# Fourth self attention without a maximum, its transposed scores in two pairs of PSUM banks in turn

## The reference, cut to what matters

```python
x = x + _L3_attn_ref(_layernorm(x, axis=-1), ...)

def _L3_attn_ref(x, Wq, bq, Wk, bk, Wv, bv, Wo, bo):
    SCALE = 1.0 / np.sqrt(D_K * 2.0)
    TEMP = 1.5
    ...
    q = _l2norm(heads(Wq, bq))
    k = _l2norm(heads(Wk, bk))
    v = heads(Wv, bv)
    scores = jnp.einsum('bhqd,bhkd->bhqk', q, k) * SCALE
    scores = jnp.clip(scores, -5.0, 5.0)
    causal = jnp.triu(jnp.ones((T, T), dtype=bool), k=1)
    scores = jnp.where(causal[None, None], -10000.0, scores)
    attn = jax.nn.softmax(scores / TEMP, axis=-1)
    out = jnp.einsum('bhqk,bhkd->bhqd', attn, v)
    out = out.transpose(0, 2, 1, 3).reshape(B, T, D)
    return (out @ Wo.T + bo) * 0.5
```

## Time and profile before

| | us |
|---|---|
| median of 3 runs | 5149.49 |
| the runs | 5117.75, 5149.49, 5162.92 |
| span of the profiled execution | 5139.5 |

### The profile page before, as it was taken

One profiled execution on the slowest core, in us unless ns is written; L12 is line 12 of the kernel. 1 busy time (PEld: TensorE's weight loads), 2 busy tenths in 40 slices (PEclk: granted clock), 3 DMA queues, 4 the chain that ended last, 5 costly groups with the idle time before them and its releaser, 6 DMA issues. The chain is left out here.

```text
span 5139.5 us, 86857 instructions
## 1 busy us (share of the span) xinstructions
PE 4115.3 (80%) x26550; PEld 2846.4 (55%) x26550; DVE 2994.6 (58%) x4577; ACT 2115.7 (41%) x3227; POOL 1733.6 (34%) x1171
## 2 busy tenths in 40 slices
PE   8899999999979988778789999994763434336699
PEld 4588888888867746534445555552432222223377
DVE  4344445444523444446545676656459999996433
ACT  3255555555522232124324555542235555551122
POOL 2266666666524232004310000000225555541033
PEclk8799999999969988799867999996876666667699
DMA  2000000000002203220022222210010101000011
GB/s 85 1 10 19 10 19 19 19 10 19 10 1 62 59 1 91 48 61 2 1 56 47 65 62 62 62 33 1 1 24 18 26 17 26 17 19 1 0 61 48
DMA packets 124607, 152.80 MB, mean 30 GB/s; under 512 B 86912, under 2 KB 110224, under 8 KB 124080
## 3 DMA queue, kind: packets, MB, share of 16 engines
q1 hardware_dynamic: 124208, 147.72, 11.5%
HBM read 109.43 MB, written 2.66 MB: 22 GB/s over the span
## 5 line engine op out<-in xcount | busy, mean ns | idle before, releaser
L989 POOL TENSOR_TENSOR pexp_lo<-arena,pexp_hi 128x800 fp32r<-128x800 f32 x384 | 635.7, 1655 | 443.2 <-POOLq L988 442.5
L2173 DVE TENSOR_REDUCE arena<-ps 100x1 f32<-100x482 f32 (+1 forms) x768 | 489.9, 657 | 266.8 <-DVEq L2160 256.5
L2053 DVE TENSOR_REDUCE arena<-ps 128x1 f32<-128x482 f32 (+3 forms) x624 | 392.9, 656 | 365.6 <-DVEq L2031 354.8
L1330 ACT ACTIVATE arena<-ps 128x800 f32<-128x800 f32 x384 | 322.3, 839 | 500.3 <-ACTq L1328 497.8
L2471 DVE MATCH_REPLACE8 arena<-arena 100x1444 f32<-100x1444 f32 x256 | 420.8, 1656 | 0.0
L1420 ACT ACTIVATE arena<-ps 128x800 f32<-128x800 f32 x384 | 315.5, 837 | 249.8 <-ACTq L1419 243.6
L3202 PE MATMUL ps<-kst,qs 96*100 96x482 f32 (+1 forms) x768 | 376.2, 492 | 43.0 <-PEq L3156 39.4
L935 POOL TENSOR_TENSOR max_diag<-w_const,arena 100x800 fp32r<-100x800 f32 x160 | 246.8, 1543 | 436.5 <-POOLq L933 436.5
L3331 PE MATMUL ps<-w_const,w_cross 100*128 100x100 f32 x192 | 43.2, 380 | 374.1 <-PEq L3328 374.1
L1331 ACT ACTIVATE pexp_hi<-ps 128x800 fp32r<-128x800 f32 x384 | 319.5, 832 | 0.0
L2573 DVE TENSOR_TENSOR arena<-ps,arena 128x400 f32<-128x400 f32 x256 | 147.1, 575 | 280.2 <-DVEq L2572 280.2
(11 more groups left out here) (393 smaller groups left out, 9621.0 us busy)
## 6 DMA issues: line engine op xcount, KB each, us to landing
ctxT<-in_ctxT SPq DMA_DIRECT2D x56, 541.5 KB
kst<-mid SPq DMA_DIRECT2D x128, 180.5 KB, 3.1
ctxk<-in_ctx SPq DMA_DIRECT2D x40, 528.0 KB
chunk<-in_ff_chunks SPq DMA_DIRECT2D x77, 193.0 KB, 2.4
arena<-gate_dram SPq DMA_DIRECT2D x64, 200.0 KB, 3.8
kst<-xn SPq DMA_DIRECT2D x64, 180.5 KB, 2.9
arena<-gate_dram SPq DMA_DIRECT2D x64, 100.0 KB, 2.6
arena<-in_ctxT SPq DMA_DIRECT2D x8, 541.5 KB
```

Source lines behind the costliest of these rows:

```text
L989: own(nc.gpsimd.tensor_tensor(pexp_lo[p % 3][:, :, :], pexp[p % 3], pexp_hi[p % 3][:, :, :], ALU.subtract))
L1330: nc.scalar.activation(pexp[p % 3], of, ACT.Exp, scale=scale).then_inc(s.pexp_ready, 1)
L2053: peak = nc.vector.tensor_reduce(mparts[0:at.stop - at.start, m, c:c + 1], bank(k, z - a, at.stop - at.start), AX.X, ALU.max)
L2173: peak = nc.vector.tensor_reduce(mparts2[:, h, c:c + 1], bank(k, z - a, S), AX.X, ALU.max)
```

## The change

Where `cfg["unit"]` is set, GpSimd leaves its part of the stage out, VectorE makes no `k_diag` and no maxima, and TensorE has a list of its own: value rows first, then in each step the values of step t - 1, the masks and transposed scores of step t + 1 (`bounded_score`, into banks 0 and 1 or 2 and 3 in turn, where ScalarE's exponent reads them), and the side work behind them. The dummies of a unit stand ahead of its first scores. The other three self attentions keep their code.

```diff
--- before.py
+++ after.py
@@ -644,6 +644,9 @@
 
     UNREAD_FIRST, UNREAD = 14, 8
 
+    def score_bank(cfg, t):
+        return 2 * (t % 2) if cfg.get("unit") else 4
+
     CHUNKS = [(0, 482), (482, 962), (962, K)]
     SCORE_BANKS, SUM_BANKS = (0, 1, 3), (2, 4)
 
@@ -918,6 +921,8 @@
 
         def self_attention(n):
             nsm = SELF[SA[n]]["nsm"]
+            if SELF[SA[n]].get("unit"):
+                return
             ident = W("const", "ident")[0:S, 0:S].unsqueeze(1).to_broadcast([S, 8, S])
 
             def own(ins):
@@ -1247,7 +1252,8 @@
                     roots()
                 act.wait_ge(s.scoresT, 1)
                 act.sem_inc(s.scoresT, -1)
-                nc.scalar.activation(probsT[:, t % 2, :].rearrange("p (c t) -> p c t", c=2), ps[0:S, 4:6, 0:GT], ACT.Exp,
+                of = score_bank(cfg, t)
+                nc.scalar.activation(probsT[:, t % 2, :].rearrange("p (c t) -> p c t", c=2), ps[0:S, of:of + 2, 0:GT], ACT.Exp,
                                      scale=float(cfg["scale"])).then_inc(s.probsT_ready, 1)
                 if t % 2 == 0 and t > 0:
                     keep(t // 2 - 1)
@@ -1759,7 +1765,9 @@
                 nc.vector.tensor_scalar(col[:, 7:8], W(wst, "gate_b"), -1.0, None, ALU.mult).then_inc(s.dve_done, 1)
                 dve.wait_ge(s.dve_done, 1)
                 dve.sem_inc(s.dve_done, -1)
-            dve.sem_inc(s.stage_pool, 1)
+            bounded = cfg.get("unit")
+            if not bounded:
+                dve.sem_inc(s.stage_pool, 1)
             dve.sem_inc(s.stage_act, 1)
             dve.sem_inc(s.stage_pe, 1)
             cols = W("const", "head_cols")
@@ -1805,7 +1813,7 @@
                     else:
                         done(nc.vector.tensor_copy(to, bank(i % 8)))
                     dve.sem_inc(s.heads_read, 1)
-                if i == 1:
+                if i == 1 and not bounded:
                     for j in range(4):
                         k_diagonal(0, j)
             if cfg.get("gate"):
@@ -1871,11 +1879,12 @@
                     done(nc.vector.tensor_tensor(xd, of, xd, ALU.add))
                     dve.sem_inc(s.proj_free, 1)
 
-            for t in range(3):
-                maxima(t)
+            if not bounded:
+                for t in range(3):
+                    maxima(t)
             for t in range(8 * units):
                 u, k = divmod(t, 8)
-                if k < 4 and u + 1 < units:
+                if k < 4 and u + 1 < units and not bounded:
                     k_diagonal(u + 1, k)
                 kind, G, i = beside(nsm, t)
                 if kind == "project":
@@ -1884,7 +1893,7 @@
                     by_roots(u // nsm - 1)
                 elif step_behind(nsm, t) == 5:
                     by_weights(u // nsm - 1)
-                if t + 3 < 8 * units:
+                if t + 3 < 8 * units and not bounded:
                     maxima(t + 3)
                 if t % 2 == 1 and t >= 3:
                     normalise(t // 2 - 1)
@@ -2755,7 +2764,18 @@
 
                 par, sm, half, at, own = place_of(t)
                 r = slice(32 * (half + c), 32 * (half + c) + 32)
-                return mm(bank(4 + c, GT, S), k_rows[sm][r, at], q_diag[par][r, :, own], start=False, stop=True)
+                return mm(bank(score_bank(cfg, t) + c, GT, S), k_rows[sm][r, at], q_diag[par][r, :, own], start=False, stop=True)
+
+            def bounded_score(t):
+
+                if t % 8 == 0:
+                    pe.wait_ge(s.q_diag_ready, 1)
+                    pe.sem_inc(s.q_diag_ready, -1)
+                    unread(UNREAD if t > 0 else UNREAD_FIRST)
+                for c in range(2):
+                    mm(bank(score_bank(cfg, t) + c, GT, S), id_bf, causalT_bf[:, :], start=True, stop=False)
+                scoreT(t, 0)
+                scoreT(t, 1).then_inc(s.scoresT, 1)
 
             def values(t):
                 u, k = divmod(t, 8)
@@ -2813,6 +2833,39 @@
                 score(t, 0)
                 score(t, 1).then_inc(s.scores, 1)
 
+            if cfg.get("unit"):
+                for i in range(4):
+                    value_rows(0, i, VALUE_BANKS[i])
+                pe.wait_ge(s.v_ready, 4)
+                pe.sem_inc(s.v_ready, -4)
+                bounded_score(0)
+                for t in range(8 * units):
+                    kind, G, i = beside(nsm, t)
+                    if t > 0:
+                        pe.wait_ge(s.probsT_ready, 1)
+                        pe.sem_inc(s.probsT_ready, -1)
+                        values(t - 1)
+                    if t + 1 < 8 * units:
+                        bounded_score(t + 1)
+                    if kind == "features":
+                        features(G, i)
+                    elif kind == "project":
+                        project()
+                    elif kind == "values":
+                        side_bank()
+                        value_rows(G, i, 7)
+                    if t % 2 == 1 and t >= 3:
+                        gathered(t // 2 - 1)
+                pe.wait_ge(s.probsT_ready, 1)
+                pe.sem_inc(s.probsT_ready, -1)
+                values(8 * units - 1)
+                pe.wait_ge(s.o_kept, 1)
+                pe.sem_inc(s.o_kept, -1)
+                gathered(4 * units - 1)
+                for c in range(nsm):
+                    features(NG - 1, c)
+                project()
+                return
             pe.wait_ge(s.k_diag_ready, 1)
             pe.sem_inc(s.k_diag_ready, -1)
             first_score(0)
```

## The result

| | before | after |
|---|---|---|
| median, 13 runs each | 5148.82 us | 5165.09 us |
| lowest, highest | 5111.75, 5270.82 | 5145.61, 5220.11 |
| span of the profiled execution | 5139.5 us | 5158.2 us |

The ratio is 1.0071 with the interval [1.0043, 1.0099]: the changed kernel is slower, by 22 to 51 us. The comparison leaves out executions far above a kernel's fastest (the profiled ones of e1, e2 and e5 further down are among these), so a ratio need not be the quotient of two medians.

What follows compares the result with a forecast made beforehand. The loop was taken as bound by what TensorE streams. Start −7.6, steps −22.3, waits gone −4, new waits +7.0 and the falling clock +22.5 made −4.4 us: 5145 from 5149.5, range 5112 to 5177.

Steps and rivals of the forecast that it cites:

- the clock is low in plain steps too: Rival: whole loop low from its first wait, dummies giving back about a quarter of 68 us; 5173 us, chance 0.16.
- held clock: Rival: TensorE keeps 2.4 GHz over the loop's new waits, so all 27 us stay; 5123 us, chance 0.22.
- the sum: Whole stage at full clock: start, steps and waits that go or come together save 26.9 us.
- the price for a loop wholly at half clock: All loop steps, value rows, gatherings and dummies at 1.2 GHz: 68 us more.
- plain steps: Loop steps counted without side work: values, masks and scores, 1.77 us instead of 2.48, and 1.46 more at 1.2 GHz.
- Part 1: Ahead of the loop: shorter VectorE chain and new order let step 1 begin 7.6 us earlier, clock returning at the dummies' end.
- Part 3: Clock falls behind features in units 2 to 4 and returns with dummies in units 2 and 3; costs 22.5 us.
- Part 2: Loop steps: shorter steps save 22.3 us, waits that go 4 us, waits that come cost 7.0 us.
- the prediction's trap: Loop scores: both pairs run side by side, so removing one pair saves no time; a pair alone takes about 0.85 us.
- The waits: Gatherings wait for bank 7 behind features (1.14 us) and project (1.2 us), three of each, 7.0 us.

Runs made afterwards that it cites:

- e1: The changed kernel with 26 instead of 14 dummies ahead of the stage's first scores; ratio to the kernel before 1.0000.
- e2: e1 with four more dummies ahead of the masks in every step; ratio to the kernel before 1.0004.
- e5: The changed kernel with features and project in bank 5, features copied behind that step's exponent, dummies in bank 4; ratio to the kernel before 0.9950.
- e9: e6 with VectorE's update behind normalise and an empty exponent on ScalarE to load the table early; ratio to the kernel before 0.9933.
- e10: e9 with no dummies at the later units; ratio to the kernel before 0.9898.
- e6: e5 with 26 first dummies instead of 14; ratio to the kernel before 0.9918.
- e7: The changed kernel with 26 first dummies and 20 instead of 8 at each later unit; ratio to the kernel before 0.9998.
- e8: e5 with 26 dummies at the start and none later; ratio to the kernel before 0.9980.
- e4: The kernel before with no dummies in this stage; ratio to the unaltered kernel before 0.9995.
- e3: The changed kernel with no dummies in this stage; ratio to the kernel before 1.0062.

## Why the prediction was wrong

The forecast was a gain of 4.4 us and the outcome a loss; what happened is the rival "the clock is low in plain steps too", in the form in which dummies give a part back. That rival was put at 5173, 24 us slower, and the part is 25.1 us longer. That the sizes agree is in part luck: at a held clock the loop gains some 9 us more than the sum (below), and the dummies gave back some 8 us (an estimate: e5's 173.1 and the new waits of 5.9, less 170.8) where a quarter of 68, 17 us, was put. Right was the price for a loop wholly at half clock, 68 us: e5 (all low) is 66.5 us above e9 (held), and 69.2 if the 12 dummies that e9 has more (7.36 − 4.67 = 2.7 us, by the starts in e1 and after) are taken off. Its condition was not right: it let plain steps lose the clock, and e1 and e10 show that they hold it.

**The step that failed** is in Part 1: "I take it to come back at the end of the dummies again", and its copy in Part 3, "to come back with the dummies at the unit's end". I took two rises, seen once each, for what 14 and 8 dummies always bring. A window of before, and the first matmul of the step behind the dummies of the earlier trace rows:

```profile
3641.00:3642.00 1.00, 1.00 (x5) 0.68 (x4) 0.00 (x0) 0.00 (x0) 0.00 (x0) 0.61 0.00 0
...
2395.55 0.84 PE L2752 MATMUL ps<-max_diag,minus_ones 100*100 100x400 f32 x2
```

In the earlier trace rows the clock rose in that window, about 4.2 us into dummies of 4.63: a near thing. In the earlier trace rows it came back behind the dummies and not, as Part 3 says, during them: it was 0.50 to 2395 and 0.55 in 2395 to 2396, so it rose when the step behind them had begun. With new steps behind them, 14 dummies brought it back in 0 of 2 profiles (after, e5), 8 in 1 of 9 units that they met at a low clock (after, e1, e5, e6), 20 in 2 of 2 (e7) and 26 in 7 of 7. In these last nine cases the rise came between 3.7 us (e8) and some 6 us (e10) behind the first dummy, and 14 are over after 4.67. A miss had cost little before, as e4 shows: the old steps, with `lower` and four strips of scores, bring the clock back with no dummies at all. The new ones don't (e3, e8). Which of the removed matmuls makes the old ones do it stays open, and so does whether the wait of 0.81 us that now stands ahead of the first dummies, where TensorE had none before, made them miss. So the fall that I had priced at 8 us for a unit, ended by the next dummies, had no end, and the first unit, which I had at full clock, was low from its start.

**Part 1, the rest.** VectorE's shorter chain shows: TensorE's wait for the normalisations fell from 30.01 us to 28.6. These 1.4 us lie ahead of the part, which doesn't hold them. The dummies began 1.55 us behind the start of the last value product, against 1.46 in the sum, and took 4.67. Masks and scores behind them took 0.81 + 1.58 = 2.39 us; the 2.4 that I had named for the other clock.

**Part 2, the steps.** Right. A pair of scores alone costs 0.85 us at full clock (3709.11 − 3708.26 in e10), as the prediction's trap said. A step without side work is 1.80 us in e10 (3709.11 − 3707.31), against 1.77; at half clock 3.25, and 1.77 + 1.46 = 3.23 was foretold. An odd step is 2.62, against 2.67. Only the value row was too dear: 2.20 − 1.80 = 0.40 us, not 0.9, as its bias, a product of one row, now runs beside the scores (3637.04 and 3637.05). Eleven of them give 5.5 us more gain at a held clock. At half clock it takes 3.92 − 3.25 = 0.67, and 1.35 was put.

**The waits.** Near: 0.88 us behind features and 1.09 behind project, where 1.14 and 1.2 stood; the six sum to 5.9 us, against 7.0. A seventh for bank 7, 0.95 at the loop's end, was there before (0.96).

**Part 3, the fall.** Right in place: in the one unit of the changed kernel that had full clock, in e1 and e2, and in three units of e7, it fell at the wait behind features or in the step after it, six times of six. The section "A second HAM failure mode: psum-queue depth-cycling" of the Trainium skill's page "TensorE: Matmul & The Clock Gate" tells of short idles between groups that make the clock swing. e7 agrees, with three falls behind waits of 0.89 us; the changed kernel hardly swung, with one return, and stayed low for the rest.

**The sum at a held clock.** −26.9 us with the waits, −33.9 without; less the 1.4 of VectorE that lie ahead of the part, −32.5. e9, which has neither waits in the loop nor falls and 12 dummies more, has a part of 106.6: −39.1, or −41.8 without these dummies. The value rows make 5.5 of the 9.3 between; the table load moved away may be a part of the rest, which no run shows by itself.

**Chances.** 0.16 for what came was too little. For the low clock spoke a window of 17 us, busy and at 0.50, in the old kernel itself; for the return spoke nothing but that I had seen it twice, without having looked how near to the dummies' end it came.

## What to carry to other kernels

When matmuls are taken out of a loop, read in the trace which clock the loop has and what brought it there: the removed work may have been what raised it, and the same streams at 1.2 GHz cost more than what was saved. A rise seen once is not a rule: look how near it came to failing, and what brings the clock back if it fails. Here it paid to raise the clock once (26 dummies did it in 7 of 7 profiles) and then to leave TensorE no wait: side work in its own bank, and the first use of a table ahead of time. Not every wait made the clock fall, but every fall came at a wait or in the step behind one, and in the two profiles without waits in the loop there was none, with a part 39 to 42 us shorter than before. Dummies in the loop were worth nothing when it had no waits (e9 0.9933 with them, e10 0.9898 without), and a patch when it had (e6 0.9918, e8 0.9980).

## What the runs showed of the hardware

- TensorE can be busy without a gap and still be granted half its clock: 138.55 of 140 us at 0.50 in e8, mostly f32 products of 32 rows and of 100x100. The same kind of stream was held at 1.00 in e10 (busy 70.95 of 71 us), where the dummies ahead had raised it and no wait came. So the busy share of a stretch doesn't tell its clock.
- In this loop, at full clock, each of six waits of 0.88 to 0.89 us was followed by a fall (after, e1, e2, e7), and two of five of 0.66 to 0.69: e6 at 0.66 and e8 at 0.69 fell, e1, e6 and e7 at 0.68 to 0.69 did not. One of 0.31 left the clock alone (e6). The old loop kept its clock over waits of 2.00 and 0.79.
- A matmul of one row issued among products of 32 rows cost nothing that can be seen: a value row took 0.40 us with it at full clock, about its 128-row product alone.
